# A two-layer local transformer on Trainium2: projections in three float32r passes, and a new order of work in its attention slot

## The reference

```python
def _layer(x, wqkv, qs, ksc, wo, lg, lb, w1, b1, w2, b2):
    h = shift_token(x)                       # half of the features comes from the token before
    qkv = h @ wqkv                           # 128 -> 3 x 512
    q, k, v = jnp.split(qkv, 3, axis=-1)     # 8 heads of 64
    ...
    q = l2norm(q) * qs
    k = l2norm(k) * ksc
    q, k = rotary_xpos(q, k)
    o = local_attention(q, k, v)             # softmax over the own and the previous 64 keys
    x = x + o @ wo
    h = shift_token(x)
    ...                                      # LayerNorm
    h = h @ w1 + b1
    a, g = jnp.split(h, 2, axis=-1)
    h = a * jax.nn.gelu(g, approximate=False)
    x = x + h @ w2 + b2
    return x
```

## Time and profile before

| | |
|---|---|
| device time, median of 3 runs | 1535.98 us (1535.06 to 1538.76) |
| profiled execution, its own time | 1539.69 us |
| its span | 1537.8 us |
| busy share of the span | PE 87%, PEld 63%, DVE 74%, ACT 52%, POOL 47% |
| stretch 800 to 1000 us (slots of layer 0) | PE 99%, DVE 92%, ACT 75%, POOL 68%, granted TensorE clock 1.00 |
| stretch 1200 to 1400 us (slots of layer 1) | PE 99%, DVE 92%, ACT 74%, POOL 68%, granted TensorE clock 1.00 |
| stretch 1000 to 1100 us (end of layer 0's slots, feed-forward) | PE 81%, DVE 58%, ACT 38%, POOL 25%, granted clock 0.95 |

### The profile page before, as it was taken

The page is one execution under the profiler, slowest core; times in us unless marked ns, Lnnn a source line. Parts: engine busy times, 40 slices in busy tenths (PEclk is TensorE's granted clock), DMA queues, the critical chain, the costliest instruction groups (busy, mean ns, idle before and its releaser), DMA issues.

```text
span 1537.8 us, 39029 instructions
## 1 busy us (share of the span) xinstructions
PE 1338.7 (87%) x15968; PEld 966.2 (63%) x15968; DVE 1145.2 (74%) x2484; ACT 799.3 (52%) x1633; POOL 724.0 (47%) x562
## 2 busy tenths in 40 slices
PE   4545999987999999994799999977889999999787
PEld 3434888875777777772466666654556666666554
DVE  4776766534888888873799999974569999999465
ACT  1222223223666666663677777743347777776321
POOL 1752455442333443334666666632146666666100
PEclk7876899996999999997999999999999999999999
DMA  4000555410000000002000100011100000000011
GB/s 135 0 0 7 111 106 112 89 30 5 3 3 3 3 3 3 3 4 89 10 9 8 22 9 9 1 30 27 24 25 10 9 14 17 9 5 5 10 37 48
DMA packets 61837, 40.34 MB, mean 26 GB/s; under 512 B 41312, under 2 KB 51808, under 8 KB 61664
## 3 DMA queue, kind: packets, MB, share of 16 engines
q1 hardware_dynamic: 61664, 37.88, 10.5%
HBM read 27.12 MB, written 2.36 MB: 19 GB/s over the span
## 4 chain that ended last, share of the span: by engine, by line
POOL 24%; DVE 8%; SPq 7%; issue 7%; PE 4%; ACT 2%; DMA 1%; DVEq 0%; POOLq 0%; ACTq 0%
POOL rot L1537 14%; POOL rn L1530 11%; SPq L1463 6%; DVE qk L1631 5%; DVE e_pm L1614 1%; PE PS L2018 1%; PE PS L2027 1%; PE PS L1962 1%; DVE e_mx L1610 1%; PE PS L1877 0%; SPq L1460 0%; SPq L1459 0%; DMA qks<-in_e_ks 0%; PE PS L1919 0%; DVE xn L1682 0%
## 5 line engine op out<-in xcount | busy, mean ns | idle before, releaser
L1537 POOL TENSOR_TENSOR rot<-qk,sinl 128x1024 f32<-128x1024 f32 x64 | 217.7, 3401 | 112.1 <-DVE qk L1631 112.1
L1530 POOL TENSOR_TENSOR rn<-ss,neghalf 128x16 f32<-128x16 f32 x64 | 185.6, 2900 | 108.5 <-DVE ss L1624 108.5
L1102 DVE TENSOR_REDUCE d_mx<-PS 128x4 f32<-128x576 f32 x128 | 96.9, 757 | 66.3 <-PE PS L1246 63.3
L1877 PE MATMUL PS<-wqkv,hT 128*128 128x512 f32 x256 | 129.7, 630 | 7.4 <-DMA qks<-in_e_ks 5.5
L1757 ACT ACTIVATE qk<-PS 128x512 f32<-128x512 f32 x128 | 76.2, 597 | 104.3 <-PE PS L1877 104.3
L607 POOL TENSOR_TENSOR uu<-uu,cb 128x512 f32<-128x512 f32 x64 | 82.7, 1294 | 90.0 <-DVE uu L839 88.5
L739 ACT ACTIVATE sg<-PS 128x512 f32<-128x512 f32 x72 | 43.0, 597 | 134.2 <-PE PS L667 134.2
L1928 PEld LDWEIGHTS PS<-ident,e_pm 128*128 128x128 f32 x512 | 58.4, 141 | 80.1 <-issue 80.1
L1165 ACT ACTIVATE pa<-PS 128x512 f32<-128x512 f32 x128 | 76.5, 597 | 61.8 <-PE PS L1255 61.7
L839 DVE TENSOR_TENSOR uu<-sg,PS 128x512 f32<-128x512 f32 x72 | 49.4, 687 | 66.8 <-ACT sg L739 66.0
L1246 PE MATMUL PS<-kx,d_q 32*64 32x256 f32 (+1 forms) x2048 | 98.0, 306 | 0.0
(11 more groups left out here) (241 smaller groups left out, 3535.1 us busy)
## 6 DMA issues: line engine op xcount, KB each, us to landing
cb<-comb_rows SPq DMA_DIRECT2D x32, 512.0 KB, 9.1
X<-in_L_attn_x SPq DMA_DIRECT2D x4, 512.0 KB, 7.1
zs<-Z SPq DMA_DIRECT2D x64, 32.0 KB
zg<-Z SPq DMA_DIRECT2D x16, 128.0 KB
out_x<-X SPq DMA_DIRECT2D x8, 256.0 KB, 2.5
zs<-Z SPq DMA_DIRECT2D x64, 31.8 KB
zg<-Z SPq DMA_DIRECT2D x16, 127.0 KB
wqkv<-in_e_wqkv SPq DMA_DIRECT2D x2, 768.0 KB, 4.3
```

Source lines behind the costliest of these rows:

```text
L1102: chain(dve.tensor_reduce(mx[:, par, :, :], s, AX.X, ALU.max))
L1530: pool.tensor_tensor(rn[:, v % 2, :], ss[:, v % 2, :], c.neghalf[:, :], ALU.pow).then_inc(rn_ready.sem, 1)
L1537: pool.tensor_tensor(rot[:, :, :, :], x, bc(sinl[:, t, :, :], 2, H2), ALU.mult).then_inc(rot_ready.sem, 1)
L1877: pe.matmul(PS[:, QBANK + s, :], h_of(v), wqkv[:, s * INNER:(s + 1) * INNER], start=True, stop=True).then_inc(eqkv_ready.sem, 1)
```

## The change

Three things are changed, all inside `local_transformer`.

1. Each of the three projections becomes three float32r matmuls: rounded features times rounded weights, rounded features times the remainder of the weights, remainder of the features times rounded weights (`project`). ACT's copy out of PSUM now writes the rounded features `h_hi`; a new DVE subtraction of 128x128 (`low`) writes the remainder `h_lo`, at the start of DVE's slot. The weights are rounded by ACT (`round_weights`, 3 pieces of 128x512 a layer); their remainder is made by DVE ahead of layer 0, ahead of the tables of sines and cosines, and by POOL (`split_weights`) in the first three feed-forward groups of layer 0 for layer 1. In the front of layer 0 `project_qk` now waits for `low`.
2. The turned tokens have another place in PSUM (behind the outputs of `weigh`), so that `turn_z` waits for `divide(v - 6, 0)`; the constants `mask32` and `zero` share memory with `hT`. The next layer's weights may be loaded earlier.
3. The order of the slot changes on three engines. On DVE both halves of `divide` and `clamp` now stand ahead of `rotated`. On PE the mask (`hide`) of the next unit moves to the end of the slot, the first half of `turn_p` to the end of its own unit's slot, and `turn_qk` goes behind the first `weigh`. On ACT `features` stands first, `squares` comes one slot later, and both `take_p` stand ahead of `exponent`. In slot 32 `up(L, 0, 0)` keeps its place ahead of what is left of `turn_p`.

The subtraction of the maxima is on DVE in both kernels.

The second `take_p` no longer stands behind the first `exponent`. The diff, cut to its core:

```diff
+        w_hi, w_lo = ssb("wqkv_hi", [P, 3 * INNER], F32R), ssb("wqkv_lo", [P, 3 * INNER], F32R)
+        h_hi, h_lo = ssb("e_h_hi", [P, 4, P], F32R), ssb("e_h_lo", [P, 4, P], F32R)
...
+        def turned_z(L, v):
+            return PS[:, QBANK, 3 * P:4 * P] if L and v < 5 else PS[:, OBANK, 3 * P:4 * P]
...
-        sp.wait_ge(ev_psum.sem, ev_psum.at(nunits * L))
+        sp.wait_ge(wlo_ready.sem, wlo_ready.at(3 * L))
...
+def split_weights(L, k):
+    pool.wait_ge(whi_ready.sem, whi_ready.at(3 * L + k + 1))
+    pool.tensor_tensor(w_lo[:, third(k)], wqkv[:, third(k)], w_hi[:, third(k)], ALU.subtract).then_inc(wlo_ready.sem, 1)
...
+def low(L, v):
+    dve.wait_ge(eh_ready.sem, eh_ready.at(n(L, v)))
+    dve.tensor_tensor(h_lo[:, v % 4, :], turned_z(L, v), h_hi[:, v % 4, :], ALU.subtract).then_inc(el_ready.sem, 1)
...
+    if has(u + 4) and (u >= 0 or L == 0):
+        low(L, u + 4)
...
         divide(L, u - 1, 0)
+        divide(L, u - 1, 1)
+    if has(u + 3):
+        clamp(L, u + 3)
     if has(u + 2):
         rotated(L, u + 2)
-    if has(u + 3):
-        clamp(L, u + 3)
-    if has(u - 1):
-        divide(L, u - 1, 1)
     if has(u - 2):
...
+for k in range(3):
+    dve.wait_ge(whi_ready.sem, whi_ready.at(k + 1))
+    dve.tensor_tensor(w_lo[:, third(k)], wqkv[:, third(k)], w_hi[:, third(k)], ALU.subtract).then_inc(wlo_ready.sem, 1)
...
+        if L + 1 < DEPTH and lead(g) is not None:
+            low(L + 1, lead(g) + 4)
...
+    act.activation(h_hi[:, v % 4, :], turned_z(L, v), ACT.Copy).then_inc(eh_ready.sem, 1)
...
+def round_weights(L, k):
+    if k == 0:
+        act.wait_ge(qkv_loaded.sem, qkv_loaded.at(16 * 3 * (L + 1)))
+        if L:
+            act.wait_ge(ev_psum.sem, ev_psum.at(nunits * L))
+    act.activation(w_hi[:, third(k)], wqkv[:, third(k)], ACT.Copy).then_inc(whi_ready.sem, 1)
...
 def attend(L, u):
-    if has(u + 4):
-        take_features(L, u + 4)
+    if has(u + 4) and (u >= 0 or L == 0):
+        features(L, u + 4)
     if has(u - 1):
         take_p(L, u - 1, 0)
+    if has(u + 3):
+        squares(L, u + 3)
+    if u == nunits - 1:
+        whole(L, 0)
+    if has(u + 4):
+        take_features(L, u + 4, 1)
+    if has(u + 4):
+        take_features(L, u + 4, 0)
+    if has(u - 1):
+        take_p(L, u - 1, 1)
+    if has(u + 2):
+        values(L, u + 2)
     if has(u):
         exponent(L, u, 0)
-    if has(u + 2):
-        values(L, u + 2)
-    if u == nunits - 1:
-        whole(L, 0)
-    if has(u - 1):
-        take_p(L, u - 1, 1)
+    if has(u - 2):
+        take_o(L, u - 2)
     if has(u):
         exponent(L, u, 1)
-    if has(u - 2):
-        take_o(L, u - 2)
     if has(u + 1):
         take_qk(L, u + 1)
-    if has(u + 5) and (u >= -1 or L == 0):
-        features(L, u + 5)
-    if has(u + 4):
-        squares(L, u + 4)
...
+    if has(v - 6):
+        pe.wait_ge(o_ready.sem, o_ready.at(2 * n(L, v - 6) - 1))
+    elif L and has(v - 4):
...
+def project(to, v, k):
+    pe.matmul(to, h_hi[:, v % 4, :], w_hi[:, third(k)], start=True, stop=False)
+    pe.matmul(to, h_hi[:, v % 4, :], w_lo[:, third(k)], start=False, stop=False)
+    return pe.matmul(to, h_lo[:, v % 4, :], w_hi[:, third(k)], start=False, stop=True)
 
 def project_qk(L, v):
-    pe.wait_ge(eh_ready.sem, eh_ready.at(n(L, v)))
-    if v == 0:
-        pe.wait_ge(qkv_loaded.sem, qkv_loaded.at(16 * 3 * (L + 1)))
-    for s in range(2):
...
+    pe.wait_ge(el_ready.sem, el_ready.at(n(L, v)))
...
+    elif has(v - 1):
+        pe.wait_ge(qk_taken.sem, qk_taken.at(2 * n(L, v - 1)))
+    for s in (1, 0):
+        if v == 0:
+            pe.wait_ge(wlo_ready.sem, wlo_ready.at(3 * L + s + 1))
+        project(PS[:, QBANK + s, :], v, s).then_inc(eqkv_ready.sem, 1)
...
+def hide(L, v):
...
 def attend(L, u):
+    if u == 0 and L:
+        hide(L, 0)
     if has(u):
         scores(L, u)
+    if u == nunits:
+        up(L, 0, 0)
     if has(u + 4):
         project_qk(L, u + 4)
-    if u == nunits:
-        up(L, 0, 0)
-    if has(u - 1):
-        turn_p(L, u - 1, 0)
-    if has(u + 2):
-        project_v(L, u + 2)
     if u == nunits - 1:
         turn_x(L, 0)
     if has(u - 1):
         turn_p(L, u - 1, 1)
+    if has(u + 2):
+        project_v(L, u + 2)
+    if has(u - 1):
+        weigh(L, u - 1, 0)
     if has(u + 1):
         turn_qk(L, u + 1)
-    if has(u - 1):
-        weigh(L, u - 1, 0)
     if has(u - 2):
         turn_o(L, u - 2)
     if has(u - 1):
         weigh(L, u - 1, 1)
+    if has(u):
+        turn_p(L, u, 0)
     if has(u - 2):
         project_o(L, u - 2)
+    if has(u + 1) and (u >= 0 or L == 0):
+        hide(L, u + 1)
```

More of the change, by code:

```diff
@@ L1433, in lead, with third @@
             return g - 7 if 3 <= g <= 6 else None
-        def h_of(v):
-            return c.hT[:, v % 2, P * (v // 2 % 2):P * (v // 2 % 2 + 1)]
+        def turned_z(L, v):
+            return PS[:, QBANK, 3 * P:4 * P] if L and v < 5 else PS[:, OBANK, 3 * P:4 * P]
+        def third(k):
+            return slice(k * INNER, (k + 1) * INNER)
         with nc.Block() as block:
@@ L1581, in _ @@
                             tables(L + 1, g)
+                            split_weights(L + 1, g)
                         if g + 2 < G:
@@ L1837, in gelu @@
                        .then_inc(gelu_ready.sem, 1)
-                features(0, 0)
+                for k in range(3):
+                    round_weights(0, k)
                 for L in range(DEPTH):
@@ L1854, in _ @@
                         gelu(L, g, 2)
+                        if L + 1 < DEPTH and g < 3:
+                            round_weights(L + 1, g)
                         if L + 1 < DEPTH and lead(g) is not None:
@@ L1861, in turn_z @@
                     t, b = tile(v)
-                    if has(v - 4):
+                    if has(v - 6):
+                        pe.wait_ge(o_ready.sem, o_ready.at(2 * n(L, v - 6) - 1))
+                    elif L and has(v - 4):
                         pe.wait_ge(qkT_ready.sem, qkT_ready.at(n(L, v - 4)))
-                    elif has(v - 1):
-                        pe.wait_ge(qk_taken.sem, qk_taken.at(n(L, v - 1)))
+                    elif L and has(v - 1):
+                        pe.wait_ge(qk_taken.sem, qk_taken.at(2 * n(L, v - 1)))
                     elif L:
@@ L1869, in turn_z @@
                     pe.wait_ge(zs_loaded[b].sem, zs_loaded[b].at(48 * (TB * L + t + 1)))
[L1870 to L1878 removed]
+                    pe.transpose(turned_z(L, v), zs[:, b, :], ident[:, :]).then_inc(zsT_psum.sem, 1)
+                def project(to, v, k):
+                    pe.matmul(to, h_hi[:, v % 4, :], w_hi[:, third(k)], start=True, stop=False)
+                    pe.matmul(to, h_hi[:, v % 4, :], w_lo[:, third(k)], start=False, stop=False)
+                    return pe.matmul(to, h_lo[:, v % 4, :], w_hi[:, third(k)], start=False, stop=True)
+                def project_qk(L, v):
+                    pe.wait_ge(el_ready.sem, el_ready.at(n(L, v)))
+                    if has(v - 4):
+                        pe.wait_ge(qkT_ready.sem, qkT_ready.at(n(L, v - 4)))
+                    elif has(v - 1):
+                        pe.wait_ge(qk_taken.sem, qk_taken.at(2 * n(L, v - 1)))
+                    for s in (1, 0):
+                        if v == 0:
+                            pe.wait_ge(wlo_ready.sem, wlo_ready.at(3 * L + s + 1))
+                        project(PS[:, QBANK + s, :], v, s).then_inc(eqkv_ready.sem, 1)
                 def project_v(L, v):
@@ L1886, in project_v @@
                         pe.wait_ge(resid.sem, resid.at(nunits * L))
-                    pe.matmul(PS[:, VBANK, :], h_of(v), wqkv[:, 2 * INNER:3 * INNER],
-                              start=True, stop=True).then_inc(ev_psum.sem, 1)
+                    if v == 0:
+                        pe.wait_ge(wlo_ready.sem, wlo_ready.at(3 * L + 3))
+                    project(PS[:, VBANK, :], v, 2).then_inc(ev_psum.sem, 1)
                 def turn_qk(L, v):
@@ L1912, in scores @@
                         pe.matmul(to[:, r, :, :], identb[:, :], bc(mask[:, min(t, 1), :], 1, 4), start=True, stop=True)
+                def scores(L, v):
+                    t, b = tile(v)
+                    pe.wait_ge(qkT_ready.sem, qkT_ready.at(n(L, v)))
+                    to = PS[:, SBANK:SBANK + 2, :].rearrange("p r (j k) -> p r j k", k=2 * W2)
                     for j in range(4):
```

26 lines of the change are left out of this document (10 added, 16 removed).

## The result

The changed kernel takes 1501.07 us (median of 4 runs, 1499.30 to 1504.82) against 1535.52 for the kernel before in the same session (1534.95 to 1538.76): ratio 0.9771, 95% interval 0.9755 to 0.9788. The forecast was 1506, range 1497 to 1523, faster with 0.92. The profiled execution took 1501.32 us, its span is 1499.5, so it stands almost on its median, while that of before (1539.69) lay 4.2 above the 1535.52 (3.7 above the 1535.98 that the prediction had); spans therefore differ by 38.3 us and medians by 34.5. The stage begins at 704.00 us in this execution and at 704.72 in that of before, so 0.7 of the 38.3 lies ahead of the changed code; the stage itself is 795.5 us long against 833.1.

The account below looks back on a forecast made before the run. It took the DVE-POOL loop (9.24 us a slot) and nearly equal PE (9.34) as bounds. Terms -11.1 - 12.7 - 9 + 3.0 = -29.8 took 1539.7 to 1509.9, then 1506 against the median; range 1497 to 1523.

Parts of the forecast that it names:

- three loops: In the slots: PE, the loop through POOL and DVE alone all meet at 8.85 to 8.88 us; 8.88 taken.
- one list of 0.64 us: DVE between `rotated` and `norm`: clamp and second division go out of the POOL loop, 0.64 us less a slot.
- `turn_p`, `hide` and the rest are moved, not changed: PE's slot: only float32r saves, 0.5 us, so PE needs at most 8.84 us.
- less where it now waits for ACT: PE's slot: besides at most 8.84 us, PE may need less where it waited for ACT; no size given.
- PE gets no shorter: Rival for PE's slots: switching between float32r and float32 costs what the pass saves; 1524 to 1526.5 us, chance 0.10.
- Way back to `low`: Slots: the path from `project_qk` round to `low` takes some 8.4 us, shorter than 8.88, so nothing is counted.
- Ends: Last slots of each layer: 2.0 us from PE's `take_p` wait and 2.5 from `turn_p`, 9 gained in all.
- Feed-forward: Feed-forward part: SP sets the pace and `split_weights` is hidden; 0 counted, up to 3 us lost if not.
- Four small DMAs hold the queue: SP in the feed-forward part: four small DMAs hold its queue 8.97 us a group; the change adds none.
- Front: Front of layer 0: `low` behind DVE's tables delays the first projection; net 3.0 us lost, bounds 1 and 5.
- Against the median: Whole kernel: the profiled execution lies 3.7 us above the median 1535.98, so 1509.9 became 1506.2.

Follow-up runs that it names:

- the two float32 versions: The changed kernel with float32 projections again, 1503.90 us; the kernel before with only both divisions and the clamp moved ahead of `rotated` on DVE, 1531.42 us.

## Why the prediction was right, and where not

- **Loops.** Right in the frame: three loops, all must shrink. `norm` to `rotated` stayed (4.73), and the rest came out at 4.08 in place of 4.14, since `low`, 0.28 long, puts the next instruction off by 0.20 as `resid_sum` does in the earlier trace rows (0.19); I had taken 0.28. So the slot is 8.81 in place of 8.88, which is the 3.7 us by which the 55 slots gained more (27.5 against 23.8). The Trainium skill ("VectorE: DVE Perf Modes", section "The DRAIN you can't avoid") says that the next instruction doesn't start until the pipe is empty, but the same section adds: "A next op that is not held starts earlier". The prediction left that out; so the 0.20 against 0.28 goes against the first sentence alone, and sums from distances between starts came out within 0.02 here (4.50 - 0.64 + 0.20 = 4.06 against 4.08).
- **What the clamp is for.** The sum was right, its reason only in part. I took both moved instructions out of one list of 0.64 us. The clamp is 0.09 of it; its move counts because it lets POOL begin the roots before the additions are over. I had left out POOL's own ring of 9.19 us, whose rows were in the chain all the time.
- **PE.** "`turn_p`, `hide` and the rest are moved, not changed" failed. The order alone took 0.38 us off PE's slot (shown by the two float32 versions), 0.15 of it the hidden wait for `take_o` that "less where it now waits for ACT" had left room for. Float32r took the forecast 0.5 more, so PE has 8.45 of work and not 8.84. It changed nothing in the sum, as the other loops end at 8.81, but here the right number was partly luck: float32r, which I held for a condition of the gain, was none. With float32r worth nothing, as in the rival "PE gets no shorter", the time is 1503.9 and not that rival's 1524 to 1526.5.
- **Way back to `low`.** Right: no wait of DVE for `features` or scores in the slots; PE waits 0.29 for `low`.
- **Ends.** 9 forecast, with bounds 0 and 12; measured 5.7 and 5.2, and 1.2 in the front of layer 1, together 12.1, 3.1 more than forecast. Of the 5.7, 0.6 is the slot between the last two rotations, which no term of the forecast held. The parts were right for layer 0: from the last rotation to the last maxima 1.7 us less (2.0 with the waits taken), from there to the last `resid_sum` 3.1 less (2.5). That both `take_p` ahead of `exponent` are its cause is shown for PE's waits by the run that takes it back; a quarter of what that run loses lies in the slots, where I had counted nothing. What the move of `turn_p` gives at the ends was not tried by itself, since taking it back lengthened every slot. Nor were the other moves tried one by one: the mask and `turn_qk` on PE, `features` and `squares` on ACT, the new place of the turned tokens.
- **Feed-forward.** Right at 0, and the pace is SP's. "Four small DMAs hold the queue" was wrong in its reason: the first of them carries over 7 of some 9 us.
- **Front.** +3.0 forecast; measured +2.0 from the start of the stage, +1.3 in the span, where 0.7 is the earlier start. The place was right (`low` behind the tables). The tables ended 1.7 us earlier in the span than before (1.0 from the start of the stage), so the first matmul started at 719.52 and not at 721.03, and six passes took 2.72 us, not 3.0; the first rotation is at 730.14, not 732.3.
- **Against the median.** The forecast was made against a profiled execution 3.7 us above its median and took this off. On the profiled times the miss is 1509.9 against 1501.3, on the medians 1506 against 1501.1. The 8.5 us of the spans are 3.7 in the slots, 3.1 at the ends and the front of layer 1, and 1.7 at the front of layer 0, of which 0.7 lies ahead of the stage; the first two terms were too small and the third too large, all on the same side, so none hid another.
